# Attention by pairs of units on TensorE: eight turns, the small turns, two scores, then the other work

## The reference, cut to what matters

```python
x = x + attention(layernorm(x), ctx, ctx, mask, wq, wk, wv, wo)
x = x + experts(layernorm(x), ...)        # top 2 of 8 experts, and a shared one

# attention, for each of 8 batch entries and 16 heads
scores = rope(q) @ rope(k).T / sqrt(32)
scores = where(mask == 0, -1e9, scores)
out = softmax(scores) @ v
return concat_heads(out) @ wo
```

## Time and profile before

| | |
|---|---|
| median of 3 runs | 1417.28 us (1417.18 to 1417.96) |
| the profiled execution | 1415.83 us, of which 1414.0 us is the span of its instructions |
| TensorE busy in the span | 1346.7 us (95%) |
| VectorE, ScalarE busy | 957.0 us (68%), 838.5 us (59%) |
| mean granted TensorE clock | 0.985 of 2.4 GHz |

### The profile page before, as it was taken

The page is one execution under the profiler, slowest core; times in us unless marked ns, Lnnn a source line. Parts: engine busy times, 40 slices in busy tenths (PEclk is TensorE's granted clock), DMA queues, the critical chain, the costliest instruction groups (busy, mean ns, idle before and its releaser), DMA issues.

```text
span 1414.0 us, 28293 instructions
## 1 busy us (share of the span) xinstructions
PE 1346.7 (95%) x8110; PEld 1030.8 (73%) x8110; DVE 957.0 (68%) x2655; ACT 838.5 (59%) x1951; POOL 581.2 (41%) x724
## 2 busy tenths in 40 slices
PE   5898999999999999999898999999999999999997
PEld 4675776767667677676476777777778888888885
DVE  6887989889798888988676666666653434334342
ACT  2788979889798897988883222222213333333332
POOL 4443434434334343342254332333334555555553
PEclk9799999999999999999999999999999999999999
DMA  6544464564554646445465222222258778885652
GB/s 204 150 147 138 128 195 144 147 196 137 181 145 142 200 139 187 145 142 157 123 192 206 84 89 90 80 78 83 75 132 213 188 194 237 231 198 103 113 76 37
DMA packets 146070, 206.62 MB, mean 146 GB/s; under 512 B 35456, under 2 KB 73088, under 8 KB 145923
## 3 DMA queue, kind: packets, MB, share of 16 engines
q1 hardware_dynamic: 124562, 166.91, 38.6%
q0 software_dynamic: 17952, 33.64, 12.8%
q10 hardware_dynamic: 3408, 4.26, 1.0%
HBM read 105.49 MB, written 69.35 MB: 124 GB/s over the span
## 4 chain that ended last, share of the span: by engine, by line
PE 73%; ACT 10%; DVE 6%; issue 4%; DMA 3%; POOL 2%; SPq 2%; POOLq 0%; DVEq 0%; ACTq 0%
PE psum L1507 14%; PE psum L1509 13%; PE psum L1508 12%; PE psum L699 7%; PE psum L814 7%; PE psum L793 6%; ACT a_probs L597 5%; ACT a_probsT L603 3%; PE psum L744 3%; PE psum L745 3%; PE psum L746 3%; DVE a_probs L961 2%; PE psum L1574 1%; PE psum L714 1%; PE psum L1603 1%
## 5 line engine op out<-in xcount | busy, mean ns | idle before, releaser
L597 ACT ACTIVATE a_probs<-a_probs,a_low 128x512 f32<-128x512 f32 x512 | 366.2, 716 | 83.7 <-DVE a_low L961 83.3
L961 DVE CUSTOM_DVE_ANT_0 a_probs<-psum,a_bias 128x512 f32<-128x512 f32 x512 | 343.8, 685 | 70.7 <-PE psum L793 67.4
L699 PEld LDWEIGHTS psum<-a_ident_r,a_probs_bits 128*128 128x128 f32 x2048 | 225.1, 142 | 88.5 <-issue 26.7
L699 PE MATMUL psum<-a_ident_r,a_probs_bits 128*128 128x128 f32 x2048 | 246.4, 244 | 15.6 <-ACT a_probsT L603 9.4
L793 PE MATMUL psum<-a_kT,a_q_stack 128*128 128x512 f32 x512 | 245.3, 480 | 13.2 <-DVE a_low L961 7.8
L603 ACT ACTIVATE a_probsT<-psum 128x512 f32<-128x512 f32 x328 | 190.0, 580 | 7.0 <-PE psum L699 6.3
L1376 POOL DMA_INDIRECT out<-b_y,b_pairs_sb x71 | 112.6, 1586 | 145.8 <-DMA out<-b_y,b_pairs_sb 83.6
L1808 DVE SCALAR_TENSOR_TENSOR b_v_hidden<-b_v_hidden,psum 128x256 f32<-128x256 f32 x71 | 29.9, 422 | 170.6 <-ACT b_v_hidden L1472 170.6
L967 DVE COPY a_probsT<-psum 128x512 f32<-128x512 f32 x184 | 126.0, 685 | 4.4 <-PE psum L699 3.3
L814 PE MATMUL psum<-a_probsT,a_v 128*32 128x512 f32 x1024 | 120.5, 611 | 0.0
L1507 PE MATMUL psum<-b_w,b_vT_hi 128*128 x284 | 116.6, 411 | 0.0
(11 more groups left out here) (218 smaller groups left out, 3027.3 us busy)
## 6 DMA issues: line engine op xcount, KB each, us to landing
b_w<-w_halves SPq DMA_DIRECT2D x16, 1536.0 KB
a_q_stack<-a_qT_hi SPq DMA_DIRECT2D x254, 64.0 KB, 2.0
a_q_stack<-a_qT_lo SPq DMA_DIRECT2D x253, 64.0 KB, 2.0
w_halves<-a_w_hi SPq DMA_DIRECT2D x96, 128.0 KB, 2.0
w_halves<-a_w_lo SPq DMA_DIRECT2D x96, 128.0 KB, 2.0
a_xT_in<-in_x_turned SPq DMA_DIRECT2D x32, 256.0 KB, 2.9
a_ctx_in<-in_ctx SPq DMA_DIRECT2D x32, 256.0 KB, 2.9
a_x_in<-in_x SPq DMA_DIRECT2D x32, 256.0 KB, 3.4
```

The lines of the kernel that those rows point to most:

```text
L597: nc.scalar.activation(probs[:, h % 2, t], probs[:, h % 2, t], ACT.Exp, bias=low[:, h % H, t:t + 1], scale=-1.0, accum_out=total[:, h // G ...
L699: last = nc.tensor.transpose(out[:, P * i:P * (i + 1)].bitcast(F32R), src(i), ident_r[:])
L961: nc.vector.tensor_tensor_reduce(probs[:, h % 2, t], psum[:, t % 2], bias[:, t], 1.0, HUGE, ALU.add, ALU.min, low[:, h % H, t:t + 1]).then ...
```

## The change

The loop on TensorE goes through the units by pairs. For the even u it turns u and u + 1, then does the small turns ("kT", "qT", "inverse") that stand beside either, then the scores of u + 6 and u + 7, and then everything else that stands beside either, in the order of the table. `line` is written in the same order, so the turning banks are dealt out anew. The lists of the other four engines keep their order.

```diff
+    TURNED = ("kT", "qT", "inverse")
+    def beside_pair(u):
+        places = [place for w in (u, u + 1) for place in PE_AT.get(w, ())]
+        return [p for p in places if p[0] in TURNED], [p for p in places if p[0] not in TURNED]
     line = []
-    for u in range(H * TT):
-        line.append(("probs", u))
-        line += [(kind, i) for kind, i in PE_AT.get(u, ()) if kind in RINGED]
+    for u in range(0, H * TT, 2):
+        turned_after, others = beside_pair(u)
+        line += [("probs", u), ("probs", u + 1)]
+        line += [(kind, i) for kind, i in turned_after + others if kind in RINGED]
...
-            for u in range(H * TT):
-                turn_probs(part, b, u // TT, u % TT)
-                if u + AHEAD < H * TT or part != "last":
-                    scores(b, par, (u + AHEAD) // TT, u % TT ^ 2)
-                beside(part, b, par, u)
+            for u in range(0, H * TT, 2):
+                turned_after, others = beside_pair(u)
+                for w in (u, u + 1):
+                    turn_probs(part, b, w // TT, w % TT)
+                beside(part, b, par, u, turned_after)
+                for w in (u, u + 1):
+                    if w + AHEAD < H * TT or part != "last":
+                        scores(b, par, (w + AHEAD) // TT, w % TT ^ 2)
+                beside(part, b, par, u, others)
```

More of the change, by code:

```diff
@@ L817, in weighted, with beside @@
                 last.then_inc(s["out_filled"], 1)
-        def beside(part, b, par, u):
-            for kind, i in stages(part, PE_AT, u):
+        def beside(part, b, par, u, places):
+            for kind, i in places:
+                if not there(part, kind, i):
+                    continue
                 if kind == "kv":
@@ L832, in beside @@
                     for t, tiles, after in OUT_STEPS:
-                        if (GH * i + GH - 1) * TT + after == u:
+                        if (GH * i + GH - 1) * TT + after in (u, u + 1):
                             weighted(b, par, i, t, tiles)
```

## The result

The changed kernel takes 1486.03 us (median of 4 runs, 1481.87 to 1491.92) where the kernel before takes 1417.37 (4 runs, 1417.18 to 1417.96): a ratio of 1.0487, interval 1.0451 to 1.0523, or 68.7 us more. I had forecast 41 more, 1458, with a range to 1478. The direction was right, the size was not, and the time lies outside the range.

What follows compares the result with a forecast made beforehand. TensorE was taken to set the pace, VectorE and ScalarE having some 13% of slack. Waits of 9.75 us an entry, 6.05 net, gave 36 for six middle entries, 4 first, 1 last: 1417.3 + 41 = 1458 us, range 1430 to 1478.

Steps and rivals of the forecast that it cites:

- The second score's wait: Pair's second score waits for `lowest` two units before, other work now behind it; 9.75 us an entry, dearest pair 1.45.
- the keys' turn: Units 34 to 48: both scores stand behind the small turn beside 35 that waits for GpSimd; 0.35 us an entry.
- the next 1.2 for the score bank: Pair 34, with no other work and a VectorE copy: the following second score waits 1.2 us for `lowest`.
- the second rotation's 1.05: Pair 26's projection chunk and VectorE's rotation delay `lowest`, so the next pair's second score waits 1.05 us.
- The 1.2 for the last residual sum: Pair 62: a second score waits 1.2 us, VectorE being held by the residual sum after the last output chunk.
- The run of eight: Eight transposes in a row on TensorE, 0.65 us to the score; gain 0.02 us a pair, 5 us in all.
- The rival that runs gain nothing: A score always takes 0.30 us, so pairs are 0.07 us worse: 18 us more, 1476 us; chance 0.04.
- The small turns: Small turns ahead of both scores: only the keys' one beside 35 was given a wait, 0.35 us an entry.
- Some of it replaces waits of today: New waits replace at most today's 3.1 us of TensorE waits an entry, which was subtracted from the sum.
- The clock: Rival: a 1.45 us wait halves TensorE's clock, 12 to 24 us an entry or two falls, 1476 us; chance 0.20.
- The ends: First entry loses 4 us, with two stretches and pair 34; last loses 1, with pairs 2, 4 and 34.
- What would show it: TensorE's waits for `lowest` grow from 4.4 to some 50 us; wrong if waits are for ScalarE's copies.

Runs made afterwards that it cites:

- the last experiment: Kernel before with pairs 10, 24 and 34 in the order turn, score, turn, score, small turns, other work; 1417.03 us against 1414.48, ratio 1.0022.
- The later rotation: Changed kernel with VectorE's rotations of query tiles 1 and 2 one unit later, beside 21 and 27; 1475.47 us, ratio 1.0426.
- turns apart: Changed kernel in the order turn, score, turn, score, small turns, other work; 1442.16 us alone, 1433.19 us with the rotations one unit later as well.
- the first experiment: Changed kernel with the small turns moved from ahead of the two scores to behind them, ahead of the other work; 1462.63 us, ratio 1.0335.
- the third: Changed kernel with runs of eight undone: turn, score, turn, score, small turns, other work of both units; 1442.16 us, ratio 1.019.
- the eight chosen pairs: Kernel before with the new paired order only at even units 2, 12, 24, 38, 44, 52, 54, 60; 1420.45 us against 1414.5, ratio 1.0048.
- the spread later: Changed kernel with ScalarE's rounding of x tile 3 and copy of group 0's spread sums moved behind its copy of tile 27; 1484.68 us, ratio 1.0489.
- three edits here: Changed kernel with ScalarE's spread copy later, 1484.68 us; entry-end wait moved to the next entry's first projection, 1485.48; spreads of groups 1 and 2 one pair later, 1496.49.

## Why the prediction was right in direction and wrong in size

The experiments make a ladder from the changed kernel back: +68.7 us; small turns behind the scores, +48.9; runs of eight undone, +28.5; other work back beside its own unit (the kernel before), 0. In the profiled executions a middle entry takes 98.1, 94.8, 92.3 and 88.6 us, so that the three parts of the change cost 3.3, 2.6 and 3.7 us of an entry, the clock included. I had priced the third and held the first two for nearly free. The ladder was climbed in one order only, and its last rung also brings back the old dealing of the turning banks and puts the small turns beside their own unit; of its 28 us, some 8 come back when the rotations go one step later (pair 22 is 1.18 us shorter in each of seven entries; the totals say 10), and the rest was not tried apart.

- **The second score's wait: right in kind and at the dear places, too large in the sum.** Pair 22 lost 1.48 us (forecast 1.45); pair 34 lost 0.37 (0.35 for the keys' turn, by a median that scatters, see the last experiment) and pair 36, where the next 1.2 for the score bank had to show, 1.16, of which 0.71 stands as a wait of one of its scores for `lowest`; the second rotation's 1.05 came out as 1.06 once the small turn was out of its way. The later rotation, alone and with turns apart, confirms the cause. Elsewhere the waits were shorter: of 0.6, 1.2 and 0.5 forecast for pairs 4, 6 and 10 came +0.37, +0.46 and +0.08. The 1.2 for the last residual sum came as a wait that the sum didn't have, of TensorE at the end of an entry (L707 for `a_x_res`, 0.79 us): pair 62 is +0.72 and pair 0 -0.29.
- **The run of eight: failed step.** On TensorE's own time it was right (0.65 us forecast, 0.64 measured; two scores 0.53 forecast, 0.51 to 0.54 measured). But I priced the run by TensorE alone, as 5 us of gain. Its first score starts a turn later, and VectorE with it: 20 us, from the first experiment to the third, part of it clock, and the eight chosen pairs show the same loss without the rest of the change. The pair of 20 is the clearest, +0.72 us, which the sum had as nothing. The rival that runs gain nothing had 18 us for another reason, the score's duration, and that reason is wrong (a second score takes 0.24 us).
- **The small turns: failed step.** The sum had one of them (0.35 us an entry for the keys beside 35). `line` dealt the turning banks anew, which the section on the change even says, and I asked for no bank when ScalarE empties it. Keys' turn and `inverse` wait 16.3 us for ScalarE with both scores behind them, and the keys' turn 6.2 more for GpSimd: 20 us by the first experiment, part of it clock. `spread`, which stands behind the scores, waits another 6.3.
- **"Some of it replaces waits of today": failed step.** I took off 3.1 us an entry, 18.6 over six. Of the 21.2 us of the earlier trace rows, the two largest kinds beside `lowest` were 10.6 us and are 10.5; only four smaller kinds (2.3, 1.7, 1.0 and the last row, 0.5) are no longer in the view. The gross sum of 9.75 us an entry is by chance close to the 9.5 measured (88.6 to 98.1, mean of six); its parts are not: by stretch +2.0, +4.6, +1.8 and +1.1 where the gross terms were 3.35, 3.15, 2.05 and 1.2.
- **The clock: a rival of 0.20 that came in part.** It fell at pair 28 in four of six entries, after a wait for a turning bank and not for the rotation. These pairs took 5.80 us in the mean, the two others 4.56: 5 us in all. Over attention at most 8.5.
- **The ends.** The first entry lost 8.0 us (forecast 4) and the last 3.1 (forecast 1); with six times 9.5 that is 68.
- **What would show it.** Waits for `lowest` were to reach some 50 us and reached 24.6, and "wrong if they are for ScalarE's copies" came half true: of 62 us of waits in that view, 26.9 are for these.

Of the busy time's 19 us, some 10 are not clock by the bound above. They are waits as well, put down as busy: the end of a matmul is modelled in the profile, and score 28 at 365.21 counts as 0.47 us long, though a second score that doesn't wait starts 0.30 after the first (390.44, of the two scores that begin there, to 390.74). So each wait hides some 0.15 us, and a short one shows no idle time at all. From 60 us to the end of attention the view lists 118 waits after and 67 before, which makes some 8 us more hidden, and 36 second scores that are not listed start over 0.32 us after the first, 7.5 us in all. Both are estimates from the steps in the trace; together they are enough for the 10.

## What to carry to other kernels

An in-order engine that shares small rings of banks with two others has its waits in a loop: before work is gathered, go through every ring that the new order touches, and ask for each bank when its reader gets to it in its own list, not only for the ring that the change is about. A run of like instructions is to be priced by when its consumer gets the first result, not by its own duration alone. And a wait that is taken out is worth only the distance to the next one: three edits here removed their wait and won nothing or lost.

## What was not expected of the hardware

The clock's fall isn't decided by the wait before it alone. The wait of 1.67 us at pair 28 stands in the changed kernel with half clock right after it in four of six middle entries, and in the kernel with the later rotation the same wait of 1.67 us passes in all six at full clock (in the first entry it does not). In the kernel with the spread later the waits of the pair are shorter (0.55, 0.17 and 0.52 us), and the clock falls there in three of six. What else differs was not tried.

One kernel's runs spread with it: the four of the changed kernel took 1481.87, 1485.33, 1486.73 and 1491.92 us at mean granted clocks of 0.984, 0.981, 0.979 and 0.972.
